# Pairs of heads take one maximum, and ScalarE makes the shift of a norm, in a two-layer decoder on one core

## The reference, cut to what matters

```python
def _layernorm(x, axis=-1, eps=1e-05):
    m = jnp.mean(x, axis=axis, keepdims=True)
    v = jnp.var(x, axis=axis, keepdims=True)
    return (x - m) / jnp.sqrt(v + eps)
...
attn = jax.nn.softmax(jnp.einsum('bhqd,bhkd->bhqk', q, k) * ATTN_SCALE, axis=-1)
out = jnp.einsum('bhqk,bhkd->bhqd', attn, v)
...
x = _layernorm(x + _L0_attn_ref(x, ...), axis=-1)
x = _layernorm(x + _L0_xattn_ref(x, ctx_768, ...), axis=-1)
x = _layernorm(x + _L0_ffn_ref(x, ...), axis=-1)
x = _layernorm(x + _L1_attn_ref(x, ...), axis=-1)
x = _layernorm(x + _L1_xattn_ref(x, ctx_768, ...), axis=-1)
x = _layernorm(x + _L1_ffn_ref(x, ...), axis=-1)
```

## Time and profile before

| | us |
|---|---|
| median of 3 runs (lowest, highest) | 1197.41 (1194.89, 1200.62) |
| profiled execution | 1199.11 |
| its span, first to last instruction | 1197.2 |
| TensorE busy | 1083.9 (91%) |
| VectorE busy | 1009.7 (84%) |
| ScalarE busy | 763.3 (64%) |
| POOL busy | 209.2 (17%) |

### The profile page before, as it was taken

One profiled execution on the slowest core, in us unless ns is written; L12 is line 12 of the kernel. 1 busy time (PEld: TensorE's weight loads), 2 busy tenths in 40 slices (PEclk: granted clock), 3 DMA queues, 4 the chain that ended last, 5 costly groups with the idle time before them and its releaser, 6 DMA issues.

```text
span 1197.2 us, 17415 instructions
## 1 busy us (share of the span) xinstructions
PE 1083.9 (91%) x6154; PEld 794.0 (66%) x6154; DVE 1009.7 (84%) x1690; ACT 763.3 (64%) x2010; POOL 209.2 (17%) x257
## 2 busy tenths in 40 slices
PE   5666789899999999999998999999999999999984
PEld 3444556675677677767686678767775877676763
DVE  3899999999999999999999999999998994333316
ACT  4445445687667866787577767787677665637534
POOL 0200010031312123131313041203121211010002
PEclk8766779999999999999999999999998999999997
DMA  6313111223343232423342143413342231000302
GB/s 224 145 35 135 42 44 52 68 39 72 71 92 89 63 81 71 119 63 71 80 104 63 32 102 78 116 33 91 85 120 36 63 62 31 1 1 10 125 15 70
DMA packets 41193, 86.70 MB, mean 72 GB/s; under 512 B 3737, under 2 KB 14970, under 8 KB 40466
## 3 DMA queue, kind: packets, MB, share of 16 engines
q1 hardware_dynamic: 27282, 60.42, 15.7%
q0 software_dynamic: 13824, 25.17, 12.1%
HBM read 54.38 MB, written 6.04 MB: 50 GB/s over the span
## 4 chain that ended last, share of the span: by engine, by line
PE 67%; DVE 19%; issue 5%; ACT 5%; POOL 3%; DMA 1%; ACTq 0%; DVEq 0%; SPq 0%; POOLq 0%
PE bank L301 20%; DVE scans L598 5%; PE bank L716 5%; PE bank L1306 4%; PE bank L764 4%; PE bank L1344 4%; PE bank L1315 4%; PE bank L982 4%; PE bank L1355 3%; PE bank L974 3%; PE bank L532 3%; PE bank L1244 3%; DVE scans L606 2%; PE bank L1338 2%; PE bank L295 2%
## 5 line engine op out<-in xcount | busy, mean ns | idle before, releaser
L561 ACT ACTIVATE scans<-dt,a_neg 128x255 f32<-128x255 f32 x512 | 224.6, 501 | 0.1
L632 POOL DMA_DIRECT2D scans<-scans x96 | 84.6, 881 | 441.6 <-DVE scans L606 441.3
L606 DVE TENSOR_TENSOR scans<-scans,BC 128x1024 f32<-128x1024 f32 x128 | 155.9, 1218 | 0.2
L598 DVE TENSOR_TENSOR_SCAN scans<-scans 128x1024 f32<-128x1024 f32 x64 | 146.1, 2282 | 6.0 <-ACT scans L561 6.0
L598 DVE TENSOR_TENSOR_SCAN scans<-scans,dBx_odd 128x1024 f32<-128x1024 f32 x64 | 146.2, 2284 | 3.0 <-ACT scans L561 2.8
L1392 ACT ACTIVATE ya<-bank,nmax 128x256 f32<-128x256 f32 x240 | 110.7, 473 | 34.2 <-DVE nmax L1459 18.3
L532 PE MATMUL bank<-ident,scans 128*128 128x128 f32 x640 | 101.4, 296 | 18.0 <-DVE scans L606 17.7
L1459 DVE TENSOR_REDUCE nmax<-bank 128x2 f32<-128x512 f32 x128 | 84.3, 683 | 36.4 <-PE bank L1306 35.9
L532 PEld LDWEIGHTS bank<-ident,scans 128*128 128x128 f32 x640 | 82.5, 153 | 37.6 <-DVE scans L606 21.9
L1401 ACT ACTIVATE ya<-bank 128x512 f32<-128x512 f32 x120 | 68.6, 604 | 21.2 <-PE bank L1315 20.6
L1306 PE MATMUL bank<-kT,qT 64*128 64x256 f32 x512 | 72.3, 402 | 5.8 <-ACT ya L1401 4.5
(11 more groups left out here) (273 smaller groups left out, 2287.5 us busy)
## 6 DMA issues: line engine op xcount, KB each, us to landing
BC<-xpj_scratch SPq DMA_DIRECT2D x31, 1024.0 KB, 6.0
scans<-scans POOLq DMA_DIRECT2D x96, 256.0 KB, 3.3
xin<-in_x SPq DMA_DIRECT2D x8, 256.0 KB, 2.8
conv<-in_x SPq DMA_DIRECT2D x8, 256.0 KB, 3.0
out<-scans SPq DMA_DIRECT2D x8, 256.0 KB, 2.1
kept_x<-x SPq DMA_DIRECT2D x7, 256.0 KB, 3.2
kept_w<-wa SPq DMA_DIRECT2D x7, 256.0 KB, 2.0
BC<-kept_w SPq DMA_DIRECT2D x1, 1792.0 KB, 8.5
```

What stands on the lines that cost most here:

```text
L561: ins = act.activation(step[:, j, 1:S], dt[b % 2][:, c, 1:S], ACT.Exp, scale=a_neg[:, c, n:n + 1])
L598: dve.tensor_tensor_scan(H, H, flat(dBx[u % 2]), 0.0, ALU.mult, ALU.add).then_inc(s["a_scan"], 1)
L606: dve.tensor_tensor(H, H, Ch, ALU.mult).then_inc(s["a_hC"], 1)
```

## The change

Both heads of a pair have their scores in two banks that now lie in one tensor (`both`), and `greatest` is one operation over 1024 columns with four results, one step of the order instead of two; it waits for the second head's scores. The exponentials of both heads wait for it. The shift goes from POOL to ScalarE (`shift`): one tiny copy with the root as scale per tile, a step of its own, then a wait for both at the start of the next step of that stream. So POOL has one instruction per norm, VectorE's string has 64 letters fewer, ScalarE's 56 more. All five strings are new. Between a norm's shift and its first normalisation ScalarE's string has other streams' steps at 21 of the 56 norms: one at 14 of them, two or more at 7.

```diff
     "act": (
-        "FFFFFFFFFFFFFSSFSSSFFSSSFFSFSFFFSSSSSSFSSFFSSFSSSSSSFFSSSSSSSSGGWFSSSSSSGGWSWWSFSWWSWSWSFFFFSWSWSSWFFWWWSWFFSW"
...
+        "FFFFFFFFFFFFFFSSFSSSSFSSFSSFFFSSFFFSFSSSSSSSSFFSSSSSSFSFSFSSFSFSSSGSGWSSSGGGFWWSWSSSSWWWWSWFFFSFWWSWFSWSSFFWWW"
...
     "dve": (
-        "FFFFFFFFFFFFSWWSSSFSSFFSFSFSSSSSWSFSFYSFSSSSSSSFSYSSFSFSFSSSFSYWYSSSSSSSSSSSWSSSSFSWSGGSSGSGGFSGSGSGWSSYSSWYSS"
-        "WYWWSWYWWFYSSSWWWFWFWFWWSYWSWWYWSSSSWFYFSWSYFWSSSWFSSFSFYWFWFWSWYWYWSSSSSYYYSSSYSFYSSYSSFYYSSFSYYFYGGSFSYSSGFG"
-        "GVGYGGYSSSSSYVYWFYFWWWWFWYWVSYSSWYWFWSWFWVYWFWYWYWFWFWYSSVSSYWYSSSVYSYWWSSSYSWSSSFYVWSSWWSWVWWWVWWVFSVVVVVSVSS"
-        "SYSYYSSWSYSSYWSWWWWWWYSSSYYSSSSSYYYGGSFSSGWSVGGYGYYGWGFWSYFVFYYSSSSWVYYYWWWWWYWVSSYFYWWWFWWFWWVWYWWSWSYFYFVFFY"
-        "WSFWSSYYWSSSWSYSSSWVSWWWFWWWVWSWVSSVVVVVVSSVSSYYYSSSWSWYSWWWSWWWYSYSFSSYSSSYSSWYSYYSSGGYSVFSSYGYGFGWGFGYGVWFSY"
-        "YSSSSYVYWYSSWYVWWWYWWFYFSSFWVWYWYWWWWWYWFWWFSYVSFYFWYFWSSVYSSSWVFSSWSSSSWSSWWVWVWWWVWWVVVSVSVSYSSYYSSSSYWSWYSW"
-        "WWWSWWYSSSSYYSSFSYSWYSGGYSYSSGVGWGWGYGGYVSSSYSSYYFSSFWVYYYWFWFWYWSWYWVYSSSWYWWYWVWWWYWWWSWFYFFVSWSSFYYFFFYWVWS"
-        "FSSWSSSSWSFSWVWWVWWWVWSWVVVVSSVVSYYSSSYSWSYSSWYWSWWWWWYSSSSYSSYSYSSGGSYWYSWGWGGSGFGGVSYSYFYFSFSFYYYWVSSWWWWVWY"
-        "WYYSSSSWYWVWYWWYWWFWFWWYWVFSYYSSSWFVFYSFWFFYYSVYWSSSWSSSVSSWSWWSVWWWWVWWSVVVVVSSSVYYYSSSFYSWSYSWWFWWWWWYSSSSSS"
-        "YYSSSGGSSYGWGGWGWGGYYSSSSSSSWYVYYWWWWWYWVFSYSWYWWSWYWVWWWWWWSYYSSWYVWSYYSSYSVYYSWSYWSVYSYSSYVWSSSWWVWWWWWWSVVS"
-        "SVVVVVVSYSYYSSSSYWSWSYWWWWWWYSSSYYSSWGYYYGWGGWGYGGGYVYWVYYYWWWWWYWVYYVYWWWYWWWYWWWWWYVYYVYWYYVWYWWWVWVVWWWWWWW"
-        "VVVVYYYVYYVYYYYYYWYVYWWWYWWWWYYYVYYYYYVYYYVYYYYVWYVWVWWWWVVVVVVVVVWWWWWWWWWWWWWWWWWW"
+        "FFFFFFFFFFFWFWSSSSSFWSSSFFSFSFSSSSSSSWSSFSFSWFSSYSSSSYSFSSFSSSSSSFSFSFSSSSSSSSSYSFWGSGSSYGFSGGSGYGSGWSSSSSWYSS"
+        "WSWYWYWFWWFSSSWWFWYWWFWWYWWWSWSSSWSSYYWSSFYFWFSYSWSSFSFWFWFSWSWYWYWFSSSSSYYYSSSYSSYFSYSFSYSSFSYYFGGFSFSGSGGSGY"
+        "GYVGSSYSSVSYWFFWWWWVWYWFSYSWSWSWFWFWVYWFWYWWFWFWSYVSSSWYSSYSVSWSWYSSSWSSSYFWVWSWSWSWVWWVWVWFSVVVVSVSVYSYYSSSSW"
+        "SYSWSWYWWSWWWYSSSYSSSYSSYGGSWSSGGFGVYGSGYGWWFVFFYSYSSSSWVYYWWWWWYWVSSYFWWWFWWFWWSWWYWVWSYFFVFWYSFFWYSSSSWSWSSS"
+        "WYSWVSWSWVWWWFWVWVSSVVVVSVSVSYYYSSSSWSSWWYWWWSWWYSYSSFSSYSSSYSWSSYGSGYSSSGVYFGGWFYGFGFGVWSYSSSYVSYWSSWWYWVWYWW"
+        "FSFSYFWWWVWYWWWWWWWSFSYFVFFYWFVSSYWSSSSVWSFWSSSSSWSWWVWVWWWVWVWVVSVSSYVYSYSSSSSYWSSWYSWWWWWWYSSSSYSSYWSSGYFGSS"
+        "YSWSGVGGWGYGGSSYSVSSYSSVWFFYYWFWFWYWSWYWVSSSYWWWYWWWWWVWWWFFSFVSWWYSSYFFYFVFWSSSFVWSSSSSWFWSWWVWWWVWSWVVVVSVVS"
+        "SYSYSSYSWSYWSSYWSWWWWWYSSSSYSSSSSGGWYSYSWGWGGSYGGGFSVYSFFSYSFVFYWSSWWVWYWYWWSSSSWWYWVWYWWWFWYWWFWSSYVFWSSSFWFV"
+        "YFYFFSSVYSWSWVSSSSWSSWWWVWWWVWWSSVVVVFSVYVSSYSYSSYSWSWFYSWWWWWWYSSSSYSSSSWGGSSSGWGGWGSGYGYSSSSSSWYYVWWWWWYWFVS"
+        "YSWWWSWWYWWVWWWWSYSSWVYSYSWYSVSYSSWYWSSYVSWSVWYSSWSWWWWVWWSVSVSVVVVSVVYSYYSYSSSWSSYWWWWWWWYSSSYSSWYGGYWWGGYGGG"
+        "GYVWVYYWWWWWYWVYYVWWWYWWWWWWWWYVYWYVYWYVWWWVWWWWWVWWWVVVVVYVYVYYYYYYWYYVYWWWWWWWYVYYVYYYVYWYYVYVYWVWWVWWVVVVVV"
+        "VVWWWWWWWWWWWWWWWWWW"
...
-    t_s_ps=NQ, t_max=NQ, t_p=2 * NQ, ...
+    t_s_ps=NQ, t_max=NQ // 2, t_p=2 * NQ, ...
...
-        bank = [ctx.enter_context(nc.psum_tensor(f"bank{i}", [P, 512], F32)) for i in range(8)]
+        bank = [ctx.enter_context(nc.psum_tensor(f"bank{i}", [P, 512], F32)) for i in range(1)]
+        both = [ctx.enter_context(nc.psum_tensor(f"both{i}", [P, 1024], F32)) for i in range(3)]
+        bank += [both[i // 2][:, i % 2 * 512:i % 2 * 512 + 512] for i in (0, 1, 2, 3, 4, 5)]
+        bank.append(ctx.enter_context(nc.psum_tensor("bank7", [P, 512], F32)))
...
-        def rstd(pool, own, tag):
-            own.link(pool.tensor_tensor(ln_rs[tag][:, :], ln_var[tag][:, :], neghalf[:, 0:T], ALU.pow))
-            return pool.tensor_tensor(ln_nb[tag][:, :], ln_nm[tag][:, :], ln_rs[tag][:, :], ALU.mult)
+        def rstd(pool, tag):
+            return pool.tensor_tensor(ln_rs[tag][:, :], ln_var[tag][:, :], neghalf[:, 0:T], ALU.pow)
+
+        def shift(act, own, tag):
+            for t in range(T):
+                own.did(act.activation(ln_nb[tag][:, t:t + 1], ln_nm[tag][:, t:t + 1], ACT.Copy, scale=ln_rs[tag][:, t:t + 1]))
+            yield
+            own.wait()
...
-        def front_act(act, b):
+        def front_act(act, own, b):
             act.wait_ge(*of("a_rstd", b, 1))
+            yield from shift(act, own, "a")
             for t in range(T):
...
-                    act.wait_ge(*of("t_max", b, h + 1))
+                    act.wait_ge(*of("t_max", b, p + 1))
...
             def greatest(p):
-                for h in (2 * p, 2 * p + 1):
-                    dve.wait_ge(*of("t_s_ps", b, h + 1))
-                    if h >= 4:
-                        dve.wait_ge(*of("t_p", b, 2 * (h - 3)))
-                    dve.tensor_reduce(nmax[:, h % 4, :], score_bank(b, h)[:, :].rearrange("p (t k) -> p t k", t=T), AX, ALU.max,
-                                      negate=True).then_inc(s["t_max"], 1)
-                    yield
+                dve.wait_ge(*of("t_s_ps", b, 2 * p + 2))
+                if p >= 2:
+                    dve.wait_ge(*of("t_p", b, 4 * (p - 1)))
+                dve.tensor_reduce(nmax[:, 2 * p % 4:2 * p % 4 + 2, :].rearrange("p h t -> p (h t)"),
+                                  both[0 if ahead(b, 2 * p) else 2][:, :].rearrange("p (n k) -> p n k", k=S), AX, ALU.max,
+                                  negate=True).then_inc(s["t_max"], 1)
+                yield
```

More of the change, by code:

```diff
@@ new lines @@
+        "YWWVWYVYSFYFVYFVYWSWYWVYVYSWYWWWWFYFWWVVYWSWYVVWWSYFYWWVVWWVVWWSWWWWWWFWVVSVVVVYFWSYYWWYSYWYYWWYWWYYSYWYWYYWSW"
+        "WSYWWYWWWWWSWWWSWGYGYGGYWSSSFVWWWVSYYWYWSWVVYYYVWWVWYYSVYWVWWWYWYWSWYVVWSWYYWWYWWVVYYWSWYWWWWWWYVVYSWWWSVVVVVV"
+        "VVYVWVSWWYYYYYWYYSWWYSWWYYWYWYYSSWYWWYWWWWWYWWWSWYSWYGGWGGVVYYWYWWWVVYYWYWWVVYYYVWVYYWYVVWYYWVVYWWWWYYWWVYVWWY"
+        "YWWVVWWVVWWVWWWWWWWWWVVVVVYWYYYYYYYWYYYWYYWYYWYWYWWYYVVYWYYWVVYWWWYYVYWWYWYVYYWWWYVVYWWWYYWVYVWVVYYVVYYVVVVVVV"
+        "VWVVWWWWWWWWWWWWWWWWWWWWWWWWWWWWWWW"
@@ L471, in front_dve, with front_pool @@
                 yield
-        def front_pool(pool, own, b):
+        def front_pool(pool, b):
             pool.wait_ge(*of("a_var", b))
-            rstd(pool, own, "a").then_inc(s["a_rstd"], 1)
+            rstd(pool, "a").then_inc(s["a_rstd"], 1)
             yield
@@ L565, in scan_act, with gate_act @@
                 yield
-        def gate_act(act, b):
+        def gate_act(act, own, b):
             for t in range(T):
@@ L572, in gate_act @@
             act.wait_ge(*of("a1_rstd", b))
+            yield from shift(act, own, "a1")
             if b >= 2:
@@ L644, in scan_pool, with gate_pool @@
                     yield
-        def gate_pool(pool, own, b):
+        def gate_pool(pool, b):
             pool.wait_ge(*of("a1_var", b))
-            rstd(pool, own, "a1").then_inc(s["a1_rstd"], 1)
+            rstd(pool, "a1").then_inc(s["a1_rstd"], 1)
             yield
@@ L768, in x_pe, with x_act @@
                         yield
-        def x_act(act, b):
+        def x_act(act, own, b):
             act.wait_ge(*of("b_cxT_ps", b))
@@ L786, in x_act @@
             act.wait_ge(*of("x_rstd", b, 1))
+            yield from shift(act, own, "b1")
             for t in range(T):
@@ L828, in x_act @@
             act.wait_ge(*of("x_rstd", b, 2))
+            yield from shift(act, own, "f1")
             for t in range(T):
@@ L927, in x_dve, with x_pool @@
             yield
-        def x_pool(pool, own, b):
+        def x_pool(pool, b):
             pool.wait_ge(*of("b_ss", b))
@@ L934, in x_pool @@
             pool.wait_ge(*of("x_var", b, 1))
-            rstd(pool, own, "b1").then_inc(s["x_rstd"], 1)
+            rstd(pool, "b1").then_inc(s["x_rstd"], 1)
             yield
             pool.wait_ge(*of("x_var", b, 2))
-            rstd(pool, own, "f1").then_inc(s["x_rstd"], 1)
+            rstd(pool, "f1").then_inc(s["x_rstd"], 1)
             yield
@@ L1080, in z_pe, with z_act @@
             yield
-        def z_act(act, b):
+        def z_act(act, own, b):
             x4, x5 = x3[b % 2], x5_last if b == NB - 1 else x3[b % 2]
             act.wait_ge(*of("z_rstd", b, 1))
+            yield from shift(act, own, "c2")
             for t in range(T):
@@ L1131, in z_act @@
             act.wait_ge(*of("z_rstd", b, 2))
+            yield from shift(act, own, "c1")
             for t in range(T):
@@ L1188, in z_dve, with z_pool @@
             yield
-        def z_pool(pool, own, b):
+        def z_pool(pool, b):
             pool.wait_ge(*of("z_var", b, 1))
-            rstd(pool, own, "c2").then_inc(s["z_rstd"], 1)
+            rstd(pool, "c2").then_inc(s["z_rstd"], 1)
             yield
             pool.wait_ge(*of("z_var", b, 2))
-            rstd(pool, own, "c1").then_inc(s["z_rstd"], 1)
+            rstd(pool, "c1").then_inc(s["z_rstd"], 1)
             yield
@@ L1409, in y_act, with v_act @@
```

(18 more changed lines are left out.)

58 lines of the change are left out of this document (27 added, 31 removed).

## The result

The changed kernel takes 1211.2 us (median of 4 runs, 1207.4 to 1212.1) beside 1197.4 for the kernel before: ratio 1.0108, 95% interval 1.0082 to 1.0133. It is slower by about 13 us; the forecast was 1189.8, the range ended at 1205. The profiled execution (1207.4, span 1205.5) is the quickest of the four.

A forecast was written before the change was run, and what follows sets the result against it. VectorE was taken as the bound up to 240 us, VectorE and TensorE to 950, TensorE after. Terms -3.2, -4.3, +0.4, -2.0, +1.5 sum to -7.6: 1199.1 becomes 1191.5, less 1.7 for the median 1189.8; range 1176 to 1205.

The forecast's parts named there:

- Orders and queues: All engines' new step orders: steps ahead of each half batch of scans differ by at most four; counted 0.
- The norms' shift: Shift on ScalarE at all norms: escapes VectorE's hold on POOL; net -3.2 us, between 0 and -9.2.
- the list of held roots: Norms with a scan directly or nearly behind the variance; root held, 3.3 us from variance to shift.
- slack: Front norms: assumed to have time to spare, so held roots there would not all reach the path.
- The early stall: Batch 1's front norm, near 47 to 61 us: VectorE waits of 3.24 and 1.06 us vanish; -4.3 us.
- The maximum: Attention loop: one maximum per head pair saves VectorE 2.0 us; later first exponential costs TensorE 1.5 us.
- Start and tail: First front norm and last c1 norm: unheld, each 0.2 us later on the path; +0.4 us.
- The slower one: Rival, attention loop: later first exponential exposed at 32 of 64 pairs costs 17.0 us; 1205.3 us, chance 0.16.
- The hold only moves: Rival, norms: roots under scans are held instead of shifts, 5.7 us more; 1195.5 us, chance 0.17.
- four signs of being wrong: 2.7 us roots before TensorE waits; over 10 us loop waits; a reduction over 1.3 us; new VectorE waits before 240 us.

The follow-up runs named there:

- x2: Kernel before with its code kept, only the changed kernel's new orders on its queues; 1217.8 us, ratio 1.0164.
- x7: Changed kernel with the orders of before on every engine up to batch 0's first attention scores, new orders after; 1193.3 us, ratio 0.9951.
- x8: Changed kernel with the new orders only up to batch 0's first attention scores, orders of before after; 1214.4 us, ratio 1.0121.
- x9: Changed kernel with batch 2's last convolution step moved ahead of the variance of batch 0's f1 norm on VectorE; 1200.4 us, ratio 1.0018.
- x3: Kernel before with only the shift moved to ScalarE, orders of before; 1189.5 us, ratio 0.9928.
- x12: Kernel before with each pair's two maxima in one VectorE step, still two operations, exponentials waiting as before; 1202.2 us, ratio 1.0030.
- x16: As x7, but two maxima in one VectorE step instead of one over two banks; 1191.5 us, ratio 0.9931.
- x6: Kernel before with only the one maximum for two heads, at the first head's place, orders of before; 1203.8 us, ratio 1.0037.
- x14: As x3, with the PSUM-reading copy of w_qk moved directly behind the variance of batch 1's front norm; 1188.6 us, ratio 0.9904.
- x15: Repeat of x3 as a control; 1190.4 us, ratio 0.9921.

## Why the prediction was wrong

**Orders and queues, counted 0.** This is the step that failed. It said that at every half batch of scans the steps ahead are equal in number or differ by at most four, so "the plan stays and places move locally". The places do move locally: the two sets of strings have done the same steps at 749 of 1245 points of TensorE's. But a local move is no small one. The new orders alone cost 1.6% (x2), and by x7 and x8 the loss, some 19 us, lies before the attention; one exchange of neighbours was worth 10.8 us, and the orders up to 170 us 7.5. What the step should have asked, for the stretch in which VectorE is full: what stands directly behind each variance, and what stands on TensorE in front of what VectorE wants next. x9 shows the first; the second shows as waits in the traces, and what it is worth in time stays open.

**The norms' shift, -3.2.** The mechanism is right and the size too small. TensorE waits for its turns behind a norm 11.5 us before (12.0 with 0.5 for xin) and 4.8 after, where 8 was forecast:

```profile
PE bank L304 <- ACT xin L297: 1.4, 3, 0.8
PE both L304 <- ACT x L297: 1.2, 2, 1.1
PE both L304 <- ACT cz L297: 1.2, 2, 0.6
PE both L304 <- ACT xb L297: 1.0, 2, 0.6
```

Alone it gains 8.6 us in x3, where these waits are 5.7 us, 6.3 less than before, most of the gain. But the list of held roots was made for the norms with a scan or product directly behind the variance, and left out f1 of batch 0, where the convolution's last step, also with two SBUF inputs, comes first. It was the one that mattered, since it stands in the stretch where VectorE is full. On the list it would have been priced at 2.74 us, a root under one scan; it took 5.47, and the earlier trace rows had one of 4.87. For fronts "slack" was taken, without a row of the first batches for it. The tiny copy was right: estimated 0.30 and 0.5 for the pair, measured 0.285 and 0.48 (line 292).

POOL's busy time falls by 27.4 us (209.2 to 181.8), not by 40: the 42.0 of shifts go, and the 56 roots grow from 51.3 to 65.7, since more of them stand under VectorE's operations.

**The early stall, -4.3.** It did not go, it moved. The root was held 2.60 us, less than the 4.87 that the step allowed; the exponentials came in time. But the step priced the way from the normalisation to the first tap at the 7.1 us of the old TensorE order. Batch 1's front after the change:

```profile
52.57 1.09 ACT L297 ACTIVATE xin<-xin,shift_a,rstd_a 128x256 f32<-128x256 f32 x2
...
57.77 1.13 PE L310 MATMUL bank<-xnT,w_in 128*128 128x256 f32 x4 [1.11 <-ACT xnT L409]
58.74 0.95 PE L310 MATMUL both<-params,wa 128*128 128x1 f32 x8
59.62 1.61 PE L1592 MATMUL both<-qT,ya 8*128 8x512 f32 x2
61.16 1.97 PE L542 MATMUL both<-ident,scans 128*128 128x128 f32 x8
62.92 1.91 PE L310 MATMUL bank<-xnT,w_in 128*128 128x256 f32 x4
...
66.81 0.87 DVE L458 SCALAR_TENSOR_TENSOR conv<-bank,conv_wh,conv 128x253 f32<-128x253 f32 x2 [2.94 <-ACT conv L420]
```

From 52.57 to 66.81 it takes 14.2 us: between the two halves of the projection stand a preparation, a fold and a sum. Of 4.3 us of waits 2.9 are there again, and 5.06 in x8 and x9, whose clock was lower here; so the term was nothing, or a loss.

**The maximum, -2.0 + 1.5.** The operation itself is as forecast, 1.218 us for an estimate of 1.21. The sum of the two terms should have been -0.5, and one maximum alone measured +4.4. From start to next start one takes 1.14 us (240.07 to 241.21), where two took 1.19: 0.05 saved and not 0.08. The later exponential adds 2 to 3 us at one line of TensorE's waits, where +1.5 was counted, and x12's 0.3%, which has no later exponential, was no term of the sum at all. After the change the two lines of the loop together wait 16.2 us, where 5.9 was before and over 10 was named as a sign of being wrong. Most of that came with the new orders, since with two maxima they wait 13.2 (x16) and 11.4 (x2).

```profile
PE both L1321 <- ACT ya L1416: 8.4, 13, 1.5
PE both L1330 <- ACT ya L1407: 7.8, 12, 1.9
```

**Start and tail, +0.4**, is too small to be seen in any of these runs.

**The rivals.** The slower one named the attention loop; 1205 was near the time and wrong about the place, since the one maximum costs 4 us (x6) and not 17. "The hold only moves" had the mechanism (a root, not the shift, is held) but priced it at 2.05 us a root in the full stretch instead of looking where VectorE is full. Three of the four signs of being wrong came true: a root of 5.47 us in front of a TensorE wait, 16.2 us at the loop's two lines, and new VectorE waits before 240 us. The last leads to the cause.

## What to carry to other kernels

In a kernel whose queues are written out by hand, new orders are not a neutral carrier of a change: run the change with the old orders first, and read an order by what stands directly behind each producer that another engine waits for. Where a small operation on GpSimd follows a VectorE result, put a VectorE step that reads PSUM or has one input behind that result: the root took 0.69 us behind a copy from PSUM (x14), and 0.69 at 162.33 in the changed kernel, behind statistics with one input. What that is worth in time has to be measured; in x14 it lay within the noise. Count a moved step by the chain it is in, on the engine that is full at that time; the number of steps moved said little here. And before a wait is put down to an order, look for it in a second trace of the same order: the 3.02 us at the broadcast and 2.1 of the 8.27 us at the rope step came and went with the clock.

## What was not expected of the hardware

A held root does not come free at the next VectorE boundary each time. Each of these roots starts 0.17 us behind the start of a VectorE operation with two inputs in SBUF. At 205.37 in x9 it ends 0.5 us behind the first of two products; at 206.00 in the changed kernel it is held through a convolution step, two products and a scan, and at 47.96 in x15 through two products and a scan. The Trainium skill (SBUF — State Buffer, "SBUF: two separate sides") says that whichever of the two operations starts first has the shared port pair for its whole instruction, and that the other blocks. The first row agrees; the other two, 5.47 and 4.87 us, are longer than any single VectorE operation there (2.28), so these roots did not get the pair at one or more of the ends of a VectorE operation. What decides it was not found.

A wait of 4.28 us on TensorE cost more than itself: the clock granted in the 25 us around it was 0.93 or 0.80, against 1.00 in x9, where the wait was 1.15, and the same five groups behind it took 6.62 or 9.12 us instead of 5.25.
